# A cross-attention kernel: scores from x F and c without forming Q and K, variances from triangular quadratic forms in row layout

## The reference, cut to what matters

```python
text_p = x @ W_text + b_text            # 512 wide
audio_p = ctx @ W_audio + b_audio       # 512 wide
Q = layer_norm(text_p, g1, beta1)
K = layer_norm(audio_p, g2, beta2)
V = audio_p
alpha = softmax(Q @ K.T / sqrt(512))
out = layer_norm((alpha @ V) @ W_out + b_out + x, g_out, beta_out)
```

## Time and profile before

| | |
|---|---|
| median of three runs | 1264.77 us (1264.68 to 1264.94) |
| the profiled execution's own time | 1264.63 us |
| its span, first to last instruction | 1262.8 us |
| TensorE busy, matmuls | 1252.0 us, 6662 |
| VectorE, ScalarE, GpSimd busy | 1079.8, 1054.0, 548.6 us |

### The profile page before, as it was taken

One profiled execution on the slowest core, in us unless ns is written; L12 is line 12 of the kernel. 1 busy time (PEld: TensorE's weight loads), 2 busy tenths in 40 slices (PEclk: granted clock), 3 DMA queues, 4 the chain that ended last, 5 costly groups with the idle time before them and its releaser, 6 DMA issues.

```text
span 1262.8 us, 22599 instructions
## 1 busy us (share of the span) xinstructions
PE 1252.0 (99%) x6662; PEld 1067.9 (85%) x6662; DVE 1079.8 (86%) x1735; ACT 1054.0 (83%) x1791; POOL 548.6 (43%) x545
## 2 busy tenths in 40 slices
PE   9999999999999999999999999999999999999997
PEld 7688888888888888888888888888888888888886
DVE  6788888898888888888988888988888888889888
ACT  7788888888888888888888888988888888888884
POOL 1132455433554434554435544335544345543356
PEclk9999999999999999999999999999999999999999
DMA  7356886776876767866668767678667688667693
GB/s 259 113 146 172 237 232 178 194 184 208 241 217 176 198 181 232 236 199 174 188 202 243 225 168 201 185 219 241 208 174 192 191 240 230 188 185 186 210 234 108
DMA packets 96645, 252.49 MB, mean 200 GB/s; under 512 B 9456, under 2 KB 25328, under 8 KB 88688
## 3 DMA queue, kind: packets, MB, share of 16 engines
q1 hardware_dynamic: 75408, 187.22, 42.2%
q0 software_dynamic: 21216, 65.02, 28.6%
HBM read 137.38 MB, written 49.81 MB: 148 GB/s over the span
## 4 chain that ended last, share of the span: by engine, by line
PE 95%; DVE 2%; ACT 2%; issue 1%; DMA 1%; SPq 0%; ACTq 0%; DVEq 0%
PE wide L374 9%; PE wide L377 9%; PE wide L378 9%; PE score L302 7%; PE score L303 7%; PE score L304 7%; PE wide L304 7%; PE wide L302 7%; PE wide L303 7%; PE wide L432 7%; PE wide L430 7%; PE wide L431 7%; PE turn L303 1%; PE turn L302 1%; PE turn L304 1%; PE turn L384 1%
## 5 line engine op out<-in xcount | busy, mean ns | idle before, releaser
L1278 POOL TENSOR_TENSOR y_rows<-y_rows,betao_row 128x512 f32<-128x512 f32 x120 | 166.6, 1388 | 338.8 <-ACT y_rows L652 226.0
L374 PE MATMUL wide<-xT_hi,wt_hi 128*128 128x512 f32 x496 | 195.8, 395 | 0.3 <-DVE xT_lo L863 0.3
L377 PE MATMUL wide<-xT_lo,wt_hi 128*128 128x512 f32 x496 | 195.8, 395 | 0.0
L378 PE MATMUL wide<-xT_hi,wt_lo 128*128 128x512 f32 x496 | 195.8, 395 | 0.0
L611 ACT ACTIVATE squares<-wide,bac_col 128x512 f32<-128x512 f32 x128 | 88.4, 690 | 77.1 <-PE wide L304 77.0
L304 PE MATMUL wide<-cT_hi,wa_lo 128*128 128x512 f32 x372 | 146.8, 395 | 0.0
L302 PE MATMUL wide<-cT_hi,wa_hi 128*128 128x512 f32 x372 | 146.8, 395 | 0.0
L432 PE MATMUL wide<-wao_hi,pcT_lo 128*128 128x512 f32 x372 | 146.7, 394 | 0.0
L430 PE MATMUL wide<-wao_hi,pcT_hi 128*128 128x512 f32 x372 | 146.7, 394 | 0.0
L303 PE MATMUL wide<-cT_lo,wa_hi 128*128 128x512 f32 x372 | 146.6, 394 | 0.0
L431 PE MATMUL wide<-wao_lo,pcT_hi 128*128 128x512 f32 x372 | 146.5, 394 | 0.0
(11 more groups left out here) (172 smaller groups left out, 3555.4 us busy)
## 6 DMA issues: line engine op xcount, KB each, us to landing
xT_in<-in_xT SPq DMA_DIRECT2D x31, 1024.0 KB, 8.6
y_rows<-in_x_rows SPq DMA_DIRECT2D x124, 256.0 KB, 4.1
y_rows<-bao_row POOLq DMA_DIRECT2D x31, 1024.0 KB, 9.4
out<-y_rows SPq DMA_DIRECT2D x124, 256.0 KB, 3.3
xT_lo<-xT_in POOLq DMA_DIRECT2D x30, 1024.0 KB, 8.9
c_kept<-in_c_rows SPq DMA_DIRECT2D x32, 768.0 KB, 6.8
cT_in<-in_cT SPq DMA_DIRECT2D x31, 768.0 KB, 8.8
p_out<-probs SPq DMA_DIRECT2D x31, 512.0 KB, 4.7
```

What stands on the lines that cost most here:

```text
L374: nc.tensor.matmul(wide[h][:], wt_hi[:, d, cols], xT_hi[:, d, :], start=(d == 0), stop=False)
L377: nc.tensor.matmul(wide[h][:], wt_hi[:, d, cols], xT_lo[:, d, :], start=False, stop=False)
L378: done = nc.tensor.matmul(wide[h][:], wt_lo[:, d, cols], xT_hi[:, d, :], start=False, stop=(d == DT - 1))
L1278: nc.gpsimd.tensor_tensor(rows, rows, betao_row[:], ALU.add).then_inc(y_ready, 1)
```

## The change

Q and K are no longer formed. With F = (centred W_text) diag(g1 g2) (centred W_audio) transposed, 512 x 384, the scores are x F c plus terms linear in x and in c, times the two reciprocal deviations; F is made once at the start (`wf_hi`, `wf_lo`), and so are the linear terms (4 columns, V = 4) and the constants.

- `project` makes x F in three banks instead of `project_k` and `project_q` with eight; `scores` contracts over 384 instead of 512.
- The variance of a token of K is c M c with M = (centred W_audio)(its transpose) / 512. `k_square` multiplies a row tile of c with the lower block triangle of M (twice the blocks off the diagonal) in rows: 128 tokens by 4 + 384 columns. VectorE multiplies with the rows of c and accumulates along the row (`k_dot`). For x it is split: `q_off` has the blocks under the diagonal and the linear columns, `q_diag` the diagonal blocks, the latter against 2x less its high part; `x_double` (ScalarE) and `add_x_lo` (GpSimd) make that from a new load of x by rows (`load_x_row`, 1 MB a step).
- GpSimd makes the columns: `make_k_out` (5 operations) and `make_q_columns` (8). The two values of each context token are needed as a row on all partitions: `store_k` writes 1024 single elements to DRAM, `load_k` reads them back broadcast over 128 partitions (512 KB).
- VectorE scales and shifts the raw scores in PSUM (`scale_scores`, `shift_scores`), then takes the maxima.
- The nine outputs, quadratic and score products pass through a ring of three banks (`turn` 0, `turn` 1, `wide` 3); output of pair i - 1 stands at the end of step i.
- The start: weights first among the loads, centring, transposes, and folds in plain float32 (`fold_k_square`, `fold_q_square`, `fold_linear`, `fold_product`), before step 0; W_audio W_out is folded within step 0.

The diff, cut to its core (most removed lines are left out; they are the functions named above):

```diff
+            def store_k(i):
+                wait_apart(sp, k_out_made, i + 1)
+                wait_apart(sp, k_rows_loaded, 16 * i)
+                sp.dma_start(k_dram.rearrange("(n p) -> p n", p=P), k_out[:],
+                             allow_slow_non_contiguous=True).then_inc(k_stored, 16)
+            def load_k(i):
+                wait_apart(sp, shifted_made, T * i)
+                wait_apart(sp, k_stored, 16 * (i + 1))
+                sp.dma_start(k_rows[:].rearrange("p n s -> p (n s)"),
+                             k_dram.partition_broadcast(P)).then_inc(k_rows_loaded, 16)
...
+                store_k(i)
+                load_k(i)
+                if late:
+                    for t in range(T):
+                        store_y(i - 2, odd, t)
+                if not last:
+                    wait_apart(sp, q_off_dotted, T * (i + 1))
+                    wait_apart(sp, x_lo_added, T * (i + 1))
+                    load_x_row(i + 1)
...
+                for t in range(0 if last else T):
+                    if late:
+                        wait_apart(sp, stored[t], 16 * (i - 1))
+                    load_x(i, odd, t)
+                if not last:
+                    wait_apart(sp, k_dotted, T * (i + 1))
+                    wait_apart(sp, c_split, T * (i + 1))
+                    load_c(i + 1)
                 if not isinstance(i, int) or i < N - 2:
                     wait_apart(sp, cT_split, CT * (i + 2))
                     load_cT(i + 2)
                 if not last:
                     store_p(i)
...
+            def k_square(i, odd, t):
...
+                elif t == 2:
+                    pe.wait_ge(y_summed, T * (i - 1))
+                if t == 3:
+                    pe.wait_ge(k_dotted, T * i + 1)
+                    pe.wait_ge(k_lin_made, T * i + 1)
+                rows = slice(t * P, (t + 1) * P)
+                for j in reversed(range(CT)):
+                    to, part = k_bank[t][:, 0:V + (j + 1) * P], slice(0, V + (j + 1) * P)
+                    hi, lo = cT_hi[odd][:, j, rows], cT_lo[odd][:, j, rows]
+                    nc.tensor.matmul(to, hi, mk_hi[:, j, part], start=(j == CT - 1), stop=False)
+                    nc.tensor.matmul(to, hi, mk_lo[:, j, part], start=False, stop=False)
+                    done = nc.tensor.matmul(to, lo, mk_hi[:, j, part], start=False, stop=(j == 0))
+                done.then_inc(k_var_done, 1)
+            def q_off(i, t):
+                if t < 2:
+                    pe.wait_ge(k_dotted, T * i + 2 + 2 * t)
+                    pe.wait_ge(k_lin_made, T * i + 2 + 2 * t)
+                else:
+                    pe.wait_ge(q_diag_dotted, T * i + t - 1)
+                rows = slice(t * P, (t + 1) * P)
+                for j in reversed(range(DT)):
+                    to, part = q_off_bank[t][:, 0:V + j * P], slice(0, V + j * P)
+                    hi, lo = xT_hi[:, j, rows], xT_lo[:, j, rows]
+                    nc.tensor.matmul(to, hi, mq_hi[:, j, part], start=(j == DT - 1), stop=False)
+                    nc.tensor.matmul(to, hi, mq_lo[:, j, part], start=False, stop=False)
+                    done = nc.tensor.matmul(to, lo, mq_hi[:, j, part], start=False, stop=(j == 0))
+                done.then_inc(q_off_done, 1)
+            def q_diag(i, t):
+                if t == 0:
+                    pe.wait_ge(k_dotted, T * i + 3)
+                    pe.wait_ge(k_lin_made, T * i + 3)
+                else:
+                    pe.wait_ge(q_off_dotted, T * i + t)
+                    pe.wait_ge(q_lin_made, T * i + t)
+                rows = slice(t * P, (t + 1) * P)
+                for j in range(DT):
+                    to = q_diag_bank[t][:, j * P:(j + 1) * P]
+                    nc.tensor.matmul(to, xT_hi[:, j, rows], md_hi[:, j, :], start=True, stop=False)
+                    done = nc.tensor.matmul(to, xT_hi[:, j, rows], md_lo[:, j, :], start=False, stop=True)
...
+                cols = slice(h * P, (h + 1) * P)
+                product(wide[h][:], [(wf_hi[:, d, cols], wf_lo[:, d, cols], xT_hi[:, d, :], xT_lo[:, d, :])
+                                     for d in range(DT)]).then_inc(t_done, 1)
+            def scores(i, odd, b):
...
+                keys = slice(b * S, (b + 1) * S)
+                for l in range(LT):
+                    rows = slice((LT * b + l) * P, (LT * b + l + 1) * P)
+                    done = product(score[b][:, l * S:(l + 1) * S],
+                                   [(tT_hi[:, d, rows], tT_lo[:, d, rows], cT_hi[odd][:, d, keys], cT_lo[odd][:, d, keys])
+                                    for d in range(CT)])
+                done.then_inc(score_done, 1)
...
+            def step(i, odd, first=False, last=False):
+                k_square(i, odd, 0)
+                k_square(i, odd, 1)
+                project(i, 0)
+                k_square(i, odd, 2)
+                k_square(i, odd, 3)
+                project(i, 1)
+                q_off(i, 0)
+                q_diag(i, 0)
+                project(i, 2)
+                for t in range(1, T):
+                    q_off(i, t)
+                    q_diag(i, t)
+                if first:
+                    for d in range(CT):
...
+                        probs_context(i, d)
+                scores(i, odd, 0)
+                scores(i, odd, 1)
+                if not first:
+                    for t in range(T):
+                        output(i - 1, t)
...
+            def x_double(i):
+                act.wait_ge(xr_loaded, 16 * (i + 1))
+                wait(act, q_diag_dotted, T * i)
+                nc.scalar.copy(x_hi[:].bitcast(F32R), x_twice[:]).then_inc(x_hi_made, 1)
+                act.wait_ge(x_hi_made, i + 1)
+                nc.scalar.mul(x_twice[:], x_twice[:], 2.0).then_inc(x_doubled, 1)
...
+            def step(i, odd, first=False, last=False):
                 j = i - 1
                 late = not isinstance(i, int) or i >= 2
+                k_linear(i, 0)
+                k_linear(i, 1)
+                t_high(i, 0)
+                k_linear(i, 2)
+                k_linear(i, 3)
                 if not last:
+                    for d in range(CT):
+                        cT_high(i + 1, 1 - odd, d)
+                t_high(i, 1)
+                q_linear(i, 0)
                 if late:
                     y_norm(i - 2, odd, 0)
+                if not first:
+                    pT_high(j)
+                t_high(i, 2)
+                q_linear(i, 1)
                 if late:
                     y_norm(i - 2, odd, 1)
+                q_linear(i, 2)
                 if late:
                     y_norm(i - 2, odd, 2)
                     y_norm(i - 2, odd, 3)
+                q_linear(i, 3)
                 if not last:
+                    for d in range(DT):
+                        xT_high(i + 1, d)
+                if not first:
+                    for d in range(CT):
+                        pc_high(j, d)
+                if first:
+                    for d in range(CT):
+                        waT_copy(d)
+                    for d in range(CT):
+                        wao_high(d)
+                elif not last:
+                    xT_minus(i + 1)
+                c_high(i)
+                exponentials(i)
+                if not last:
+                    x_double(i + 1)
...
+            def dot(of, factor, rows, to):
+                return nc.vector.scalar_tensor_tensor(out=of, in0=of, scalar=factor, in1=rows, op0=ALU.mult,
+                                                      op1=ALU.mult, accum_out=to)
+            def k_dot(i, t):
+                dve.wait_ge(k_lin_made, T * i + t + 1)
+                if t == 0:
+                    dve.wait_ge(c_loaded, 16 * (i + 1))
+                    wait(dve, k_out_made, i)
...
+            def q_diag_dot(i, t):
+                dve.wait_ge(q_diag_done, T * i + t + 1)
+                dve.wait_ge(x_lo_added, T * i + t + 1)
...
+            def scale_scores(i, b):
+                dve.wait_ge(score_done, NB * i + b + 1)
+                if b == 0:
+                    dve.wait_ge(q_const_made, i + 1)
+                    wait_apart(dve, k_rows_loaded, 16 * (i + 1))
+                for l in range(LT):
+                    at = LT * b + l
+                    nc.vector.scalar_tensor_tensor(out=score[b][:, l * S:(l + 1) * S], in0=score[b][:, l * S:(l + 1) * S],
+                                                   scalar=q_add[:, at:at + 1], in1=k_rows[:, 0, b * S:(b + 1) * S],
+                                                   op0=ALU.add, op1=ALU.mult).then_inc(scaled, 1)
...
+            def step(i, odd, first=False, last=False):
                 j = i - 1
                 late = not isinstance(i, int) or i >= 2
+                k_dot(i, 0)
+                k_dot(i, 1)
                 if late:
+                    for t in range(T):
+                        y_stat(i - 2, odd, t)
+                    for t in range(T):
+                        y_moment(i - 2, t)
```

(112 more changed lines are left out.)

1143 lines of the change are left out of this document (526 added, 617 removed).

## The result

1455.66 us, median of three runs (1452.35 to 1457.52), against 1264.77: ratio 1.1505, 95% interval 1.1472 to 1.1538. Slower, as forecast, but by 191 us and not by 68, above the range. The profiled execution took 1452.35 us, its span is 1450.5.

What follows compares the result with a forecast made beforehand. TensorE's matmul spacing bounds the kernel: start 62.5 + 31 steps x 40.22 (1246.8) + end 22.2 = 1331.5 us of span, plus 1.8, gives 1333 us. Range from 1305 (narrow matmuls at 0.10) to 1385.

Steps and rivals of the forecast that it cites:

- the price of a narrow matmul: TensorE's steps: each of 68 narrow matmuls costs 0.112 us, the turn of its weight load.
- the sign: Whole kernel: slower 92%, faster 7%, the same 1%; 1333 us forecast, 5.4% slower.
- A: Narrow matmuls on TensorE: load hides wholly, they cost only their columns; step 36.3 us, time 1212; chance 6%.
- A2: Narrow matmuls on TensorE: load hides in part, 5.7 us for the 68; step 38.3, time 1274; chance 3%.
- C: Narrow fp32r matmuls on TensorE: twice float32's rate, 0.22 us for 56; 6 us a step, 1520; chance 4%.
- the step: Steady step: TensorE's 260 matmuls sum to 40.22 us, 1.8 more than 38.44.
- the end: After the last scores: 22.2 us, the rest as before, with the casts (1.5) left open.
- no engine as the bound: Other engines in a step: VectorE 25 to 27 us, ScalarE 21, GpSimd 28; none reaches 40.
- the cover: Transfers and waits within a step: all hidden behind TensorE's work, costing nothing; where it fails, each us a step is 31.
- rival B: Ring of banks: new wait, add_xT or q_const late or x_double pushing GpSimd; 1340 to 1400 us; chance 24%.
- folds in plain float32 at 0.84 ns a column: Start and step 0: squares of q 4.3 us, linear 3.1, product 5.2, 16 folds in step 0 6.9.
- the start's 31.4: Before step 1: forecast to begin at 62.5 us, 14 later than before; measured 93.9, a difference of 31.4.

Runs made afterwards that it cites:

- e4: Changed kernel with k_out turned by VectorE's block transposition and stored in four transfers of 8 runs of 128 bytes; 1365.23 us.
- e1: Changed kernel with k's columns stored as 128 runs of 32 bytes, so the factors reach the wrong tokens; 1367.05 us.
- e18: e1 with its store by rows repeated four times, each waited for before k_rows is loaded; 1442.81 us.
- e7: Changed kernel storing 512 instead of 1024 single elements of k's columns from step 1 on; 1439.67 us.
- e16: e1 with its store by rows repeated once and waited for before k_rows is loaded; 1366.9 us.
- e10: e9 with the split of P moved behind tile 2 of q on ScalarE and VectorE; 1376.19 us.
- e9: e4 with q's diagonal blocks 0 to 2 merged into q_off, and x_hi and its correction made only for the 128 columns still used; 1312.0 us.

## Why the prediction was wrong

Right: the price of a narrow matmul, 0.112 us, and with it the sign (the rivals A, A2 and C fall with the 0.11 us rows); the step, 40.22 against 39.99; the end, 22.2 against 23.0; no engine as the bound (ScalarE 21.0, GpSimd 25.7, VectorE 28.0 us in the step at 571.0; in an undisturbed one of e4 VectorE takes 30.9, above my 25 to 29).

Wrong, the larger: the cover that the forecast gave every transfer, with nothing for it in the sum. "store_k and load_k lie between 15 and 25. [...] Cover is there everywhere, so these edits cost nothing." I looked at the buffers each transfer fills, not at SyncE's queue behind them. 1024 single elements "at the same cost per byte" hid that their landing, 10 to 12 us where the same bytes as rows land in 4.8, is a wait in the queue. It eats the 3.3 us of slack before x_twice and most of the 6.9 before c_kept; in the step at 571.0 x_twice goes out at 30.9 us of it instead of 25.6 (e1), y_rows' loads behind it land after 9.2 us instead of 6.3, next to those of c_kept, cT and P's store, and P is back at 18.5 us where I had 10. In more of the steps it is c_kept, late itself, that stops TensorE at k_square 3: the first dot product, which the forecast had at 2.1 us of the step, begins at 8.7 in the one at 394.2. The price of the whole: 94 us, of which e1 and e4 give back about 89 and e18 shows 76 by the hold alone; 6 are step 1's wait for ScalarE, which the forecast did not have either.

This is rival B's kind, a new wait, but not its place: I named the ring, add_xT and q_const, and 1.5 us a step. xT_lo was 12.6 us of TensorE's 72 idle ones. The forecast also had no price for what follows a wait: 34.8 us of the 87 are added busy time, some 26 of them (an estimate) matmuls at the lower clock.

Wrong, the smaller: "folds in plain float32 at 0.84 ns a column". This is the rate of one instruction, and a call is two. Squares of q 8.7 us for 4.3, linear terms and constants 7.3 for 3.1, product 12.6 for 5.2, folds in step 0 13.4 for 6.9: 22.5 us of the start's 31.4, some 3 of them the granted clock of 0.87 and 0.80. 6.4 more lie before the squares (they begin at 19.8, not 13.4: means, centring and transposes took longer), 2.5 at the transposes in step 0. The error was in reading and the earlier trace rows: I took line 451's four matmuls for four calls. One slip changed nothing: narrow matmuls at 0.10 us give 1308, not the range's 1305.

## What to carry to other kernels

When an edit adds a wait to a queue, find the queue's slack (its waits for engines) ahead of each transfer behind the new wait, and compare the first of these with the landing time of what it now waits for, taken for that shape of transfer: here slack further back, before c_kept, did not help. Store many short columns as rows or transposed on an engine, since 4 KB in single elements can cost more than 0.75 MB of a load (89 us against 17 here). Count instructions in the trace, not calls in the code, before pricing a kind of matmul for the first time.

## What the runs showed of the hardware

- Behind a store of 1024 single floats the next transfer, which waited for its landing, went out 9.5 to 12.7 us after it (changed kernel). A store of 512 landed in 10.2 us (e7), the 4 KB of 1024 in 128 runs of 32 bytes in 4.8 (e1), and in 1.5 when it was repeated right behind (e16).
- Behind one idle gap of 2.2 us TensorE's granted clock was 0.53 over 11 us, and the step lost 7.0. It is not so behind every gap: from 461.92, behind one of 2.04 us, the clock stayed at 1.00 over 11 us.
- A plain float32 matmul is two instructions in the trace, of 512 columns 0.43 us apart (eight in 3.60 us at 86.13, one 0.59).
- A subtraction of VectorE that reads two tiles of SBUF took 4.83 us instead of 0.69 when GpSimd's four subtractions (4.22 us) had begun beside it (e10); the same operation with one operand in PSUM stayed at 0.69 in the changed kernel, e9 and e10, beside work of GpSimd too. The Trainium skill (SBUF — State Buffer, "SBUF: two separate sides") says that such an operation and one of GpSimd lock each other out of a shared port. The trace agrees, with the addition that VectorE waited for all four.
